# Attended rows evicted by ScalarE unscaled, and multiplied by the gates' row on GpSimd

## What is computed

```python
mod = (silu(c) @ wmod).reshape(8, 6, 1, 512)
sa, ca, ga, sb, cb, gb = (mod[:, i] for i in range(6))
ga = (2 * (ga >= 0) - 1) * maximum(abs(ga), 0.25)         # gb likewise
h = layernorm(x) * (1 + ca) + sa
q, k, v = ((h @ W + b).reshape(8, 16, 32, 1024) for W, b in ((Wq, bq), (Wk, bk), (Wv, bv)))
attn = softmax(einsum('bhdt,bhds->bhts', k, v) * temperature)
out = einsum('bhdt,bhts->bhds', q, attn).reshape(8, 1024, 512)
x = x + ga * out                                          # the gate and the residual
h = layernorm(x) * (1 + cb) + sb
# per batch: the 512 rows of h with the highest scores h @ w_router go through
# W1, gelu, W2 and are weighted by sigmoid(score); f is h plus these
x = x + gb * f
```

## Time and profile before

| | us |
|---|---|
| median of 3 runs | 2283.25 (2282.88 to 2284.57) |
| the profiled execution, its own time | 2283.22 |
| its span (first to last instruction) | 2281.5 |
| busy PE, DVE, ACT, POOL | 2212.2, 1890.5, 1431.7, 1398.7 |
| first phase, from the first `gated` to the last | 59.7 to 1595.8 |

### The profile page before, as it was taken

One profiled execution on the slowest core, in us unless ns is written; L12 is line 12 of the kernel. 1 busy time (PEld: TensorE's weight loads), 2 busy tenths in 40 slices (PEclk: granted clock), 3 DMA queues, 4 the chain that ended last, 5 costly groups with the idle time before them and its releaser, 6 DMA issues.

```text
span 2281.5 us, 35224 instructions
## 1 busy us (share of the span) xinstructions
PE 2212.2 (97%) x12410; PEld 840.0 (37%) x12410; DVE 1890.5 (83%) x2887; ACT 1431.7 (63%) x2478; POOL 1398.7 (61%) x1174
## 2 busy tenths in 40 slices
PE   6899999999999999999999999997899999999998
PEld 2233333333333333333333333331344444444443
DVE  6899999999999999999999999999873664563533
ACT  3688887888888888888888888888221111111110
POOL 6677887777888778887788877871642212302300
PEclk9999999999999999999999999999999999999999
DMA  7343344343335434444433533443432122112210
GB/s 255 79 104 88 92 108 96 95 103 95 91 90 122 84 93 114 85 101 100 98 89 89 127 82 91 97 84 94 139 88 70 41 66 70 61 47 70 68 31 19
DMA packets 218864, 206.06 MB, mean 90 GB/s; under 512 B 139256, under 2 KB 139288, under 8 KB 218176
## 3 DMA queue, kind: packets, MB, share of 16 engines
q1 hardware_dynamic: 208176, 174.12, 32.4%
q0 software_dynamic: 9728, 25.23, 3.5%
q10 hardware_dynamic: 784, 4.47, 0.5%
HBM read 71.37 MB, written 43.19 MB: 50 GB/s over the span
## 4 chain that ended last, share of the span: by engine, by line
PE 54%; DVE 32%; POOL 4%; issue 3%; SPq 3%; ACT 3%; DMA 1%; POOLq 0%; DVEq 0%; ACTq 0%
DVE nmax L1142 22%; PE sc L848 14%; PE sc L835 14%; PE sc L645 9%; PE acc L694 9%; PE pj L669 6%; POOL x L1530 3%; PE pj L657 3%; ACT probs L916 2%; DVE qn L1194 2%; DVE stats L1176 2%; DVE dot_out L1162 2%; SPq L480 1%; SPq L488 1%; DVE x L1171 1%
## 5 line engine op out<-in xcount | busy, mean ns | idle before, releaser
L916 ACT ACTIVATE probs<-sc,nmax 128x1024 f32<-128x1024 f32 x1024 | 1139.3, 1116 | 238.7 <-DVE nmax L1142 228.7
L1142 DVE TENSOR_REDUCE nmax<-sc 128x1 f32<-128x1024 f32 x1024 | 1206.1, 1212 | 28.3 <-PE sc L645 25.6
L694 PE MATMUL acc<-probs,qn 128*32 128x512 f32 x4096 | 546.6, 606 | 5.0 <-DVE x L1171 2.8
L1018 ACT ACTIVATE probs<-sc,b_col 128x512 f32<-128x512 f32 x128 | 87.9, 687 | 532.6 <-PE sc L835 519.1
L657 PE MATMUL pj<-room 128*128 128x512 f16 x1500 | 387.5, 381 | 2.7 <-POOL room L1483 2.7
L848 PE MATMUL sc<-room,probs 128*128 128x512 f16 x1536 | 355.5, 382 | 7.0 <-DVE probs L1362 4.1
L645 PE MATMUL sc<-room 128*128 128x512 f16 x1024 | 309.1, 384 | 23.1 <-ACT probs L916 13.7
L645 PE MATMUL sc<-stacks 128*128 128x512 f16 x1024 | 308.3, 383 | 11.7 <-ACT probs L916 10.2
L1360 DVE CAST probs<-probs 128x512 f16<-128x512 f32 x128 | 60.4, 472 | 292.1 <-ACT probs L1018 291.9
L848 PEld LDWEIGHTS sc<-room,probs 128*128 128x128 f16 x1536 | 150.8, 98 | 191.3 <-DVE probs L1362 5.0
L657 PEld LDWEIGHTS pj<-room 128*128 128x128 f16 x1500 | 144.2, 98 | 187.7 <-ACT room L887 12.2
(11 more groups left out here) (168 smaller groups left out, 2238.6 us busy)
## 6 DMA issues: line engine op xcount, KB each, us to landing
stacks<-room SPq DMA_DIRECT2D x512, 64.0 KB, 2.0
room<-room SPq DMA_DIRECT2D x508, 64.0 KB, 2.0
h_rows<-hbuf SPq DMA_DIRECT2D x132, 128.0 KB, 2.3
out<-base SPq DMA_DIRECT2D x132, 128.0 KB, 2.4
room<-in_L_attn_x SPq DMA_DIRECT2D x96, 128.0 KB, 2.6
rows<-mod_rows SPq DMA_DIRECT2D x32, 256.0 KB, 4.2
room<-in_L_ffn_W SPq DMA_DIRECT2D x8, 1024.0 KB, 5.3
probs<-in_L_wmod ACTq DMA_DIRECT2D x4, 1024.0 KB, 12.0
```

The costliest lines, as they stand in the source:

```text
L694: mm = nc.tensor.matmul(acc[at:at + DH, :], qn[:, (p // 2) % 2, p % 2, h2, :], probs[:, (2 * p + h2) % PROBS, half * D:(half + 1) * D], st ...
L916: nc.scalar.activation(probs[:, u % PROBS, :], slot(b, g, ring_at(p, h2)), ACT.Exp, bias=nmax[:, u % PROBS:u % PROBS + 1], accum_out=rsum[ ...
L1018: nc.scalar.activation(g32[:, f % 2, :], ff[f % 2], ACT.Gelu_apprx_tanh, bias=b1_col[:, f:f + 1], scale=1.0 / WS).then_inc(gelu_done, 1)
L1142: nc.vector.tensor_reduce(nmax[:, u % PROBS:u % PROBS + 1], slot(b, g, ring_at(p, h2)), AX.X, ALU.max, negate=True).then_inc(max_done, 1)
```

## The change

DVE's `gated` is gone. ACT gets `attended`: after `exp_unit(.., 0)` of steps 3 and 11 (and after whatever stands between the two exponentials of that step, as `evac_kv` in step 11), it copies `acc` into `x2` and signals `acc_free`. `residual` on POOL becomes two instructions, a multiplication of both halves by the gates' row and the addition, with a semaphore `s_gate` between them. SP loads the gates' row of a batch after group 0's `x2_done`, and POOL waits for it at group 1.

```diff
@@ sync
-                    if g == 0:
-                        if b == 0:
-                            store_modulation()
-                        sp.wait_ge(acc_free, b * (GB * SUBS) + 2)
-                        sp.dma_start(rows[:, 0, :], mod_rows[b, 0].partition_broadcast(P)).then_inc(s_ga, 16)
+                    if g == 0 and b == 0:
+                        store_modulation()
...
                     sp.wait_ge(x2_done, b * GB + g + 1)
                     if not (last and g >= GB - 3):
                         load_x((g + 3) % 4, ahead[g])
+                    if g == 0:
+                        sp.dma_start(rows[:, 0, :], mod_rows[b, 0].partition_broadcast(P)).then_inc(s_ga, 16)
@@ scalar
+            def attended(b, g, s):
+                act.wait_ge(pv_done, pair_no(b, g, s * NQ + NQ - 1) + LAG)
+                if s == 0 and b * GB + g >= 1:
+                    act.wait_ge(post_done, b * GB + g)
+                nc.scalar.activation(x2[g % 2][:, s, :], acc[:], ACT.Identity).then_inc(acc_free, 1)
...
+                        if p == 3:
+                            attended(b, g - 1, 1)
+                        if p == 11:
+                            attended(b, g, 0)
                         exp_unit(b, g, p, 1)
...
             body(LAST, True)
+            attended(B, -1, 1)
             high_part(2)
@@ vector
-            def gated(b, g, s):
-                dve.wait_ge(pv_done, pair_no(b, g, s * NQ + NQ - 1) + LAG)
-                if g == 0 and s == 0:
-                    dve.wait_ge(s_ga, b * 16 + 16)
-                nc.vector.tensor_tensor(x2[g % 2][:, s, :], acc[:], rows[:, 0, :], ALU.mult).then_inc(acc_free, 1)
...
-                        if p == 3:
-                            if b == 0 and g == 0:
-                                dve.wait_ge(s_modc, 1)
-                            gated(b, g - 1, 1)
-                        if p == 11:
-                            if end:
-                                dve.wait_ge(post_done, NG - 1)
-                            gated(b, g, 0)
                         row_max(b, g, p, 1)
...
-            gated(B, -1, 1)
@@ gpsimd, residual
                 pool.wait_ge(acc_free, b * (GB * SUBS) + g * SUBS + 2)
+                if g == 1:
+                    pool.wait_ge(s_ga, b * 16 + 16)
+                nc.gpsimd.tensor_tensor(x2_b[:], x2_b[:], rows[:, 0:1, :].broadcast_to([P, SUBS, D]), ALU.mult).then_inc(s_gate, 1)
+                pool.wait_ge(s_gate, b * GB + g + 1)
                 nc.gpsimd.tensor_tensor(x2_b[:], x2_b[:], xt[(g + 3) % 4][:], ALU.add).then_inc(x2_done, 1)
```

More of the change, by code:

```diff
@@ L349, in block_phases @@
         x2_done = sem("x2_done")
+        s_gate = sem("s_gate")
         s_bn2 = sem("s_bn2")
```

## The result

The changed kernel takes 2423.11 us in the median of 4 runs (2420.01 to 2427.8), the kernel before, run beside it, 2283.91 us (2282.88 to 2284.6, 4 runs). The ratio is 1.0612 (95% interval 1.0598 to 1.0627), so the change costs 6.1%, or 139 us. It lies inside the range, 18 us above the forecast of 2405. The profiled execution took 2420.01 us, its span is 2418.2.

The account below looks back on a forecast made before the run. PE and DVE in turns were taken to bound the kernel. 30 groups of 4.24 us give 127.2, less 2.9 and 5 hidden, plus 2.5 for group 31: 121.8 on 2283.22 makes 2405 us, range 2380 to 2436.

Parts of the forecast that it names:

- POOL's multiplication: Step 5: DVE's statistics already wait for POOL, so multiplication 2.36 plus semaphore 0.20 delays them 2.56 us per group.
- step 3's eviction on DVE's chain: Step 3: ACT's copy behind the exponential delays PE, then DVE's maximum by 0.57; 0.24 comes back, net 0.33 us.
- step 11's eviction: Step 11: ACT's copy behind exponential and `evac_kv` makes PE's products of step 12 wait 1.35 us per group.
- a full group: Sum of the three costs per full group, 2.56 + 0.33 + 1.35 = 4.24 us, times 30 is 127.2.
- hidden by the slower loop: Taken off: group 6's load wait, 2.9 us, and 5 us of extra DVE work near the groups' end.
- up to group 1: Start of the program: no loss, as DVE's load wait in group 0 hides the later step 5.
- group 31 and behind: Group 31's evictions in steps 3 and 11 behind weight conversions: 2.5 us for both, between 1 and 5.
- group 0: DVE stands 6.63 us at step 9 for a load hanging on SP, which hides the later step 5.
- The relief of DVE that the page seems to promise: Rival: DVE's relief counts and POOL's work is covered, saving 15 us, so 2268; chance 0.03.
- the evictions weren't free: Denies the rival that ACT's evictions cost nothing, leaving 1.97 us per group, 59 in all, so 2342; chance 0.12.
- the first rival: DVE's relief counts, POOL's work is covered: slot waits of 0.5 us x 30 = 15 saved, 2268; chance 0.03.
- the third rival: POOL's new instruction also holds up DVE, one `qn` per group: up to 29 us more, 2434; chance 0.08.

## Why the prediction was near, and where it was short

In its own steps, with what the runs measured:

| step of the prediction | predicted | measured | from |
|---|---|---|---|
| POOL's multiplication | 2.56 | 2.43 | POOL's starts, 909.20 and 911.63; 2.41 as the part alone |
| step 3's eviction on DVE's chain | 0.33 | 0.53 | end of `qn` after the exponential: 4.59, now 5.12 |
| step 11's eviction | 1.35 | 1.49 | table; eviction apart 1.49 |
| a full group | 4.24 | 4.45 | |
| hidden by the slower loop | -7.9 | about -9.0 | below |
| clock | none | about +4.2 | three groups |
| up to group 1 | 0 | +1.9 | first exponentials of step 3, above |
| group 31 and behind | +2.5 | +6.1 | below |
| in all | 121.8 | 136.7 | |

The range held because the mechanism was right. The 15 us by which the sum is short come from many terms: 6 from the group, 4 from the clock, 2 from group 0 and 4 from group 31, less 1 that was hidden besides.

**The three terms.** Each was on the path, as said. POOL's was 0.13 too large: the semaphore between two own instructions costs 909.20 + 2.36 to 911.63, so 0.07 us, and not the 0.20 that I had taken from another pair of instructions. ACT's two were too small, by 0.20 and 0.14. I had let PE start at the end of ACT's copy. The copy of step 11 ends at 932.17 and PE's products start at 932.31; in step 3 it is 905.60 and 905.74: 0.14 for the signal, each time. The remaining 0.06 in step 3 I can't place. The relief of DVE that the page seems to promise didn't appear, and the evictions weren't free.

**What was predicted for single rows.** PE's wait in step 12 is 1.42 (said 1.35), in step 4 0.81 (0.7), DVE's idle time for PE in step 4 is 1.19 (1.2), `qn` in step 4 takes 0.29 again (0.29). DVE's wait for POOL is 2.58, where I had said 2.9. Of the 0.32 too much, 0.13 is the gap above; DVE reaches the statistics later by the rest: its two row maxima in between take 2.50 in place of 2.34.

**What is hidden.** The kernel before needs 10.6 us more than 30 times 47.41. The changed kernel needs 5.8 more than 30 times 51.86, and 4.2 of these are the three slow stretches of the clock, so about 1.6 are left of the 10.6. The step that hides this was sized nearly right (7.9 said, 9.0 found). Most of it lies in two groups: group 6, with its load, took 51.8 and now takes 52.2, and group 9 took 49.8 and now takes 52.0. That the rest is extra work of DVE was argued and not shown.

**A reading that was wrong.** The 11.1 us that PE waits for slots were spread over all groups, 0.5 each. But 7.9 of them lie in group 31, from 1550 to 1600:

```profile
PE sc L645 <- ACT probs L916: 7.9, 10, 1.8
```

From 400 to 1550 it is 3.7 us in 14, 0.15 a group, by this view. What a full group could really give back is 47.41 less 47.01, so 0.40, as the kernel with the addition in two halves shows. The price of the first rival was near that by luck.

**The clock** wasn't in the prediction. The new pause of PE of 1.84 us, the third row of waits above, is DVE's lateness arriving at PE, and three times in 30 the clock fell behind it. It costs little in this kernel, but 19 to 24 falls cost some 25 to 30 us in two of its variants, with shorter groups. The Trainium skill (TensorE: Matmul & The Clock Gate, HAM oscillation — how this bites in real kernels) tells that PE's idle times between bursts can take it back to the lower clock over and over; the trace agrees, with 0.50 granted behind such pauses. By the rule of thumb in that section of the Trainium skill, though, idle times as short as the 1.84 us here would be harmless; in this trace three of them weren't, and the trace decides. I should have asked of every new wait of PE whether the clock stands it.

**The step that failed outright is group 0**, which I had put at nothing since DVE waits 6.63 us for a load there. I took the load as fixed. It isn't: it stands on SP behind the storing of the modulation, which waits for DVE's `base`, and that is the third rival, POOL's hold on a DVE instruction with two inputs in SBUF. The changed kernel's rows of POOL, DVE and SP's queue:

```profile
70.31 2.42 POOL L1531 TENSOR_TENSOR x<-x,xt 128x1024 f32<-128x1024 f32 x1
```

```profile
70.54 2.73 DVE L1170 SCALAR_TENSOR_TENSOR base<-hbuf 64x512 f32<-64x512 f32 x1
...
91.40 0.69 DVE L1075 BATCH_NORM_STATS2 stats<-xt 128x6 f32<-128x512 f32 x1 [5.96 <-DMA xt<-in_L_attn_x]
```

```profile
73.30 1.30 SPq L510 DMA_DIRECT2D mod_rows<-base  x4
...
86.18 2.37 SPq L442 DMA_DIRECT2D xt<-in_L_attn_x  x4
```

The same instruction without POOL's multiplication:

```profile
69.53 0.68 DVE L1170 SCALAR_TENSOR_TENSOR base<-hbuf 64x512 f32<-64x512 f32 x1
```

`base` lasts until POOL's addition is over (73.27 against 72.73), the storing starts at 73.30 where it was 71.04 before, the load follows, and DVE's statistics stand at 91.40 in place of 89.08. That rival was right in group 0 and wrong in the full groups: there no DVE instruction of the kind meets POOL's new one, and `qn` takes 0.32 us in the mean of 100 to 1550 against 0.37 before.

**The other term that was too small is group 31.** I had put 2.5 us for its two evictions behind weight conversions, between 1 and 5, and it is 6.1. The one of step 11, with PE behind it:

```profile
1713.30 1.90 ACT L964 ACTIVATE room<-room 128x2048 f16<-128x2048 f32 x1
1715.10 0.58 ACT L926 ACTIVATE x<-acc 128x512 f32<-128x512 f32 x1
```

```profile
1715.83 1.94 PE L694 MATMUL acc<-probs,qn 128*32 128x512 f32 x8 [3.31 <-ACT x L926]
```

PE waits 3.31 us there and 3.38 in step 4, where full groups have 1.42 and 0.81. The clock was also at its lower level for 6.8 us, from 1685.2 on; how the 6.1 divide between the two was not tried.

## What to carry to other kernels

Spare time of an engine over the whole program says nothing about a place where another engine already waits for it: even a wait of 0.30 us there means that whatever is put in front costs its full duration. An eviction that frees a buffer for PE should stand ahead of long work on its engine, not behind it (0 against 2.03 us per group here). Where a consumer takes a tile in halves, produce and signal it in halves: that one split was worth 0.5% here, and no engine move tried was worth anything beyond it. With the evictions ahead and the split, the moved multiplication still cost 0.3%; only with half of it done earlier was nothing of its cost left.

## What the runs showed of the hardware that I had not expected

TensorE's granted clock fell from 1.00 to 0.50 for about 3.4 us behind pauses of PE of 1.8 to 2.5 us in a program where PE is over 90% busy, between 100 and 1500 us 3 times in the changed kernel and 6, 14, 17 and 22 times in the variants with such a pause in each group. In the kernels whose groups mostly pause PE for 1.4 us or less it fell there at most once, and then behind a pause of 3.5 to 4.3 us in group 6; single pauses of 1.7 to 2.5 us in them brought no fall. Each fall cost from 1.1 us of a group (with the evictions ahead) to 1.6 (with the multiplication alone), and 1.4 in the changed kernel.

A DVE instruction with two SBUF inputs doesn't show a wait when POOL's instruction shuts it out; it shows as a longer duration, to 0.15 to 0.54 us past the end of POOL's instruction: 0.68 became 2.73, and 0.29 became 1.36 and 1.62. The Trainium skill (SBUF — State Buffer, Who interferes with whom) has the rule that such an instruction and a GpSimd instruction that reads SBUF exclude each other for the whole instruction. These three and the `qn` of 0.53 agree with it.

The gap of POOL for a semaphore between its own two instructions was 0.07 us here and 0.20 elsewhere in the same kernel; why they differ was not tried.
